# A fused eight-stage transformer kernel on one core: centring folded into weights, the exp mask moved to GpSimd, new interleaving tables

## The reference, cut to what matters

```python
# causal attention, three times (16 heads of 8 features)
scores = einsum('bhqd,bhkd->bhqk', Q, K) / sqrt(dk)
scores = where(causal, scores, NEG)
e = exp(scores - max(scores));  attn = e / e.sum(-1);  out = attn @ V
# the last three blocks
h = x
for blk in range(3):
    y = qlora_linear(h, ..., biases[2*blk])          # w = dequant(q) + lora, plus a bias
    y = layernorm(y, gamma[blk], beta[blk])           # (y - mean(y)) * rsqrt(var + eps) * g + b
    y = gelu(y)
    y = qlora_linear(y, ..., biases[2*blk + 1])
    h = y + h
x = x + h
```

## Time and profile before

| | |
|---|---|
| median of three runs | 3342.96 us (3331.83 to 3349.52) |
| span of the profiled execution, first to last instruction | 3337.4 us |
| device time of the profiled execution | not shown apart; the median is 5.6 us above the span |
| PE busy | 2641.8 us (79%) |
| ACT busy | 1912.7 us (57%) |
| DVE busy | 1763.9 us (53%) |
| POOL busy | 3.6 us |
| mean granted TensorE clock | 0.795 of full speed |

### The profile page before, as it was taken

One profiled execution on the slowest core, in us unless ns is written; L12 is line 12 of the kernel. 1 busy time (PEld: TensorE's weight loads), 2 busy tenths in 40 slices (PEclk: granted clock), 3 DMA queues, 4 the chain that ended last, 5 costly groups with the idle time before them and its releaser, 6 DMA issues.

```text
span 3337.4 us, 46425 instructions
## 1 busy us (share of the span) xinstructions
PE 2641.8 (79%) x18736; PEld 1529.0 (46%) x18736; DVE 1763.9 (53%) x2698; ACT 1912.7 (57%) x1960; POOL 3.6 (0%) x12
## 2 busy tenths in 40 slices
PE   8999999777997789877898688986889868897215
PEld 4666456343563435534355344553445534453102
DVE  5463574545656355553555545654455544563524
ACT  2433435875358753586445864468534685447994
POOL 0000000000000000000000000000000000000000
PEclk7997989659896588966899668986779867987557
DMA  3000000000000000000000000000000000000000
GB/s 128 2 1 1 20 1 1 1 1 8 1 1 1 1 8 1 1 1 0 8 1 1 1 0 8 2 1 1 0 5 2 1 1 0 4 1 1 0 0 6
DMA packets 4561, 18.68 MB, mean 6 GB/s; under 512 B 608, under 2 KB 864, under 8 KB 3808
## 3 DMA queue, kind: packets, MB, share of 16 engines
q1 hardware_dynamic: 4320, 15.38, 1.2%
HBM read 13.28 MB, written 2.10 MB: 5 GB/s over the span
## 4 chain that ended last, share of the span: by engine, by line
PE 54%; ACT 19%; DVE 15%; issue 12%; DVEq 0%; DMA 0%; ACTq 0%; SPq 0%
ACT back_cosines L1320 6%; PE one_ps L1164 2%; PE two_ps L1275 2%; PE one_ps L862 2%; PE two_ps L910 2%; ACT back_cosines L1322 2%; PE one_ps L1710 2%; DVE back_nsum L1330 2%; PE one_ps L1717 2%; ACT L1320 2%; PE one_ps L766 1%; PE one_ps L1723 1%; DVE back_cosines L1393 1%; ACT L1862 1%; PE two_ps L862 1%
## 5 line engine op out<-in xcount | busy, mean ns | idle before, releaser
L1320 ACT ACTIVATE back_cosines<-back_cosines 128x2048 f32<-128x2048 f32 x256 | 472.2, 1899 | 0.5
L933 ACT ACTIVATE front_scratch<-one_ps 128x1152 f32<-128x1152 f32 x168 | 171.5, 1021 | 225.0 <-PE one_ps L848 224.8
L1322 ACT ACTIVATE back_cosines<-back_cosines,wts 128x2048 f32<-128x2048 f32 x128 | 252.4, 1994 | 41.1 <-DVE back_cosines L1393 40.9
L1330 DVE TENSOR_REDUCE back_nsum<-back_cosines 128x8 f32<-128x2048 f32 x64 | 144.4, 2281 | 234.0 <-ACT back_cosines L1320 234.0
L797 DVE TENSOR_REDUCE front_negm<-one_ps 128x8 f32<-128x1024 f32 (+1 forms) x168 | 204.4, 1220 | 56.6 <-PE one_ps L772 55.5
L837 PE MATMUL one_ps<-ident_bf,mask_q 128*128 128x256 bf16 x480 | 93.3, 302 | 80.5 <-ACT front_scratch L933 69.3
L696 ACT ACTIVATE back_cosines<-two_ps,wts 128x512 fp32r<-128x512 f32 x28 | 19.3, 688 | 224.1 <-PE two_ps L910 224.1
L766 PE MATMUL one_ps<-front_qkr 32*128 32x128 f32 (+1 forms) x896 | 136.5, 414 | 14.1 <-issue 8.9
L1393 DVE TENSOR_SCALAR back_cosines<-two_ps 128x2048 f32<-128x2048 f32 x56 | 128.2, 2290 | 28.5 <-PE two_ps L1257 28.3
L933 ACT ACTIVATE back_cosines<-two_ps 128x1152 f32<-128x1152 f32 (+1 forms) x84 | 86.0, 1024 | 92.0 <-PE two_ps L848 92.0
L766 PEld LDWEIGHTS one_ps<-front_qkr 32*128 32x128 f32 x896 | 96.6, 274 | 88.5 <-DVE front_negm L797 46.3
(11 more groups left out here) (630 smaller groups left out, 5795.1 us busy)
## 6 DMA issues: line engine op xcount, KB each, us to landing
wts<-w_dram SPq DMA_DIRECT2D x1, 4184.0 KB, 15.3
front_xin<-x_dram SPq DMA_DIRECT2D x8, 256.0 KB, 4.2
out_dram<-back_z SPq DMA_DIRECT2D x8, 256.0 KB, 2.1
wts<-w_dram SPq DMA_DIRECT2D x1, 1736.5 KB, 19.1
wts<-w_dram SPq DMA_DIRECT2D x1, 1199.0 KB, 5.3
wts<-w_dram SPq DMA_DIRECT2D x1, 1152.0 KB, 16.5
wts<-w_dram SPq DMA_DIRECT2D x3, 256.0 KB, 5.8
wts<-w_dram SPq DMA_DIRECT2D x1, 516.5 KB, 4.8
```

Of the source, the lines that this page charges most:

```text
L933: nc.scalar.activation(h.probs[:, e % 2, 0:n * HEADW].rearrange("p (k c) -> p k c", c=HEADW), h.ps[:, 0:n, 0:HEADW], ACT.Exp, scale=float( ...
L1320: nc.scalar.activation(cosines, cosines, func, scale=scale).then_inc(h.arc_pass.sem, 1)
L1322: nc.scalar.activation(cosines, cosines, func, scale=scale, bias=C(bias)).then_inc(h.arc_pass.sem, 1)
L1330: nc.vector.tensor_reduce(h.nsum[:, kt, :].rearrange("p (g2 j) -> p j g2", g2=2), h.cosines[:, u % 2, kt * 4 * TOK:(kt + 1) * 4 * TOK].rea ...
```

## The change

1. In the causal stages the mask matmuls of the score sets are gone. The exponential is taken of unmasked diagonals, written in another arrangement (for each set, first the tiles of key tile 0 on the diagonal, then the off-diagonal ones, then the other diagonal ones, so that key tile 0 of a head is two pieces 2n tiles apart in PSUM order and n tiles in SBUF order), and GpSimd then sets what lies above the diagonal to zero with one `affine_select` for each set over the 2n diagonal tiles. A new semaphore `probs_kept` stands between GpSimd and the PV matmuls. The scores of the next set still wait for `probs_ready` of ACT alone.
2. In the three blocks the first weight is centred once (`weff` minus its mean over the output features), and its bias with it. The bias step on DVE and the centring matmul of each block go; ACT squares the PSUM result with the centred bias added, and DVE adds the bias in the normalising product. The prologue gets one small matmul, one copy, one reduction and one more pass over half of `weff`. The DMA of the `qlora` parameters is issued ahead of `lora` and gets a semaphore of its own.
3. All interleaving tables are new, and there is one for GpSimd.

```diff
-         "arccos", "qlora", "block0_in", "block0", "block1_in", "block1", "block2_in", "block2"]
+         "arccos", "qlora", "block0", "block1", "block2"]
...
-    "block0": ("y", "xn", True, "eps5", "block0_in", None),
+    "block0": ("y", "xn", False, "eps5", None, None),
...
 PE_RUNS = {
     "fronts": (
-        1, 1, 1, 1, 1, 1, 1, 1, 1, 1, 2, 2, 2, 1, 2, 2, 5, 1, 5, 2, 1, 1, 2, 1, 2, 1, 2, 1, 2, 1, 2, 1, 2, 2, 2,
+        1, 2, 1, 1, 1, 1, 1, 1, 1, 1, 1, 1, 1, 1, 2, 1, 2, 1, 2, 1, 3, 1, 5, 1, 1, 1, 1, 1, 2, 1, 6, 1, 3, 1, 1,
...
+POOL_RUNS = {
...
+    "both": (
+        12, 12, 12,
+    ),
...
+        def score_tile(h, k, kt):
+            return h.ps[:, k, 0:HEADW].rearrange("p (n q) -> p n q", q=P)[:, 0:3:2, :] if kt == 0 else h.ps[:, k, P:2 * P]
+
+        def prob_tile(h, e, k, kt):
+            n = TRIOS[e % len(TRIOS)]
+            tiles = h.probs[:, e % 2, 0:n * HEADW].rearrange("p (t k q) -> p t k q", k=n, q=P)
+            return tiles[:, 0:3:2, k, :] if kt == 0 else tiles[:, 1, k, :]
+
         def causal_scores_pe(pe, h, turn, s):
...
-                    for k in range(len(heads)):
-                        diagonals = h.ps[:, k, :].rearrange("p (n q) -> p n q", q=P)[:, 0:4:2, :]
-                        nc.tensor.matmul(diagonals, mask_q[:], ident_bf[:].unsqueeze(1).broadcast_to([P, 2, P]),
-                                         start=True, stop=False, skip_group_check=True)
-                    for kt, into in ((0, slice(0, SEQ)), (1, slice(SEQ, HEADW))):
+                    for kt in range(2):
...
         def causal_pv_pe(pe, h, turn, s, e):
...
-            pe.wait_ge(h.probs_ready.sem, h.probs_ready.at(turn, s, e + 1))
+            pe.wait_ge(h.probs_kept.sem, h.probs_kept.at(turn, s, e + 1))
...
-                nc.scalar.activation(h.probs[:, e % 2, 0:n * HEADW].rearrange("p (k c) -> p k c", c=HEADW),
-                                     h.ps[:, 0:n, 0:HEADW], ACT.Exp, scale=float(HD) ** -0.5).then_inc(h.probs_ready.sem, 1)
+                nc.scalar.activation(h.probs[:, e % 2, 0:n * HEADW].rearrange("p (t k q) -> p k t q", k=n, q=P),
+                                     h.ps[:, 0:n, 0:HEADW].rearrange("p k (t q) -> p k t q", q=P), ACT.Exp,
+                                     scale=float(HD) ** -0.5).then_inc(h.probs_ready.sem, 1)
+
+        def causal_keep_pool(pool, h, turn, s):
+            for e in range(CSETS):
+                n = TRIOS[e % len(TRIOS)]
+                yield
+                pool.wait_ge(h.probs_ready.sem, h.probs_ready.at(turn, s, e + 1))
+                pool.sem_inc(wait_carrier)
+                diagonals = h.probs[:, e % 2, 0:2 * n * P].rearrange("p (n q) -> p n q", q=P)
+                nc.gpsimd.affine_select(diagonals, diagonals, pattern=[[0, 2 * n], [1, P]], compare_op=ALU.is_ge, fill=0.0,
+                                        base=0, channel_multiplier=-1).then_inc(h.probs_kept.sem, 1)
...
         def block_pe(pe, h, turn, s):
...
-            yield from norm_pe(pe, h, turn, s)
+            yield
+            pe.wait_ge(h.norm_sq.sem, h.norm_sq.at(turn, s))
+            nc.tensor.matmul(h.ps[:, 1, :], C("mean"), h.sq[:], start=True, stop=True).then_inc(h.norm_var.sem, 1)
...
         def block_act(act, h, turn, s):
...
-            yield from norm_act(act, h, turn, s)
+            yield
+            act.wait_ge(h.lin_ps.sem, h.lin_ps.at(turn, s, 1))
+            nc.scalar.activation(h.sq[:], h.ps[:, 2, :], ACT.Square, bias=centred_bias[:, i:i + 1]).then_inc(h.norm_sq.sem, 1)
...
         def block_dve(dve, h, turn, s):
...
-            dve.wait_ge(h.lin_ps.sem, h.lin_ps.at(turn, s, 1))
-            nc.vector.tensor_scalar(h.y[:], h.ps[:, 2, :], bias[:, 2 * i:2 * i + 1], None, ALU.add).then_inc(h.resid.sem, 1)
-            yield from norm_dve(dve, h, turn, s)
+            yield
+            dve.wait_ge(h.norm_rstd.sem, h.norm_rstd.at(turn, s))
+            nc.vector.scalar_tensor_tensor(out=h.xn[:], in0=h.ps[:, 2, :], scalar=centred_bias[:, i:i + 1], in1=h.sq[:],
+                                           op0=ALU.add, op1=ALU.mult).then_inc(h.norm_out.sem, 1)
...
             load_x(0, slice(2 * TOK, 3 * TOK))
+            load("qlora")
             load("lora")
             sp.dma_start(weff_int[:], qw_dram).then_inc(qint_loaded, 16)
-            load("qlora")
...
+            pe.wait_ge(*weights_of("qlora"))
+            last = nc.tensor.matmul(two_back.ps[:, 1, 2 * P:2 * P + 3], C("centre"), W("qlora", "bias")[:, 0:6:2], start=True, stop=True)
             last.then_inc(lora_ps, 1)
...
-                .then_inc(weff_ready, 1)
+                .then_inc(dequant_step, 1)
+            nc.vector.tensor_copy(centred_bias[:], two_back.ps[:, 1, 2 * P:2 * P + 3]).then_inc(dequant_step, 1)
+            dve.wait_ge(dequant_step, 5)
+            first_linear = weff[:].rearrange("p (n c) -> p n c", c=P)[:, 0:6:2, :]
+            nc.vector.tensor_reduce(weff_sum[:], first_linear, AX.X, ALU.add).then_inc(dequant_step, 1)
+            dve.wait_ge(dequant_step, 6)
+            nc.vector.scalar_tensor_tensor(out=first_linear, in0=weff_sum[:].unsqueeze(2).broadcast_to([P, 3, P]), scalar=-1.0 / P,
+                                           in1=first_linear, op0=ALU.mult, op1=ALU.add).then_inc(weff_ready, 1)
```

More of the change, by code:

```diff
@@ L86 @@
 LOADS = {"const": ("const",), "masks": ("masks",), "first": ("causal0",), "moe0": ("moe0",), "front": ("causal1", "mqa", "moe1"),
-         "lora": ("lora",), "back": ("qlora", "linear"), "late": ("causal2", "mlp", "arccos")}
+         "lora": ("lora",), "qlora": ("qlora",), "back": ("linear",), "late": ("causal2", "mlp", "arccos")}
 def columns():
@@ L294, in __init__ @@
         self.front, self.region, self.passes = parts is FRONT, region, passes
-        if not self.front:
-            stages |= {f"block{i}_in" for i in range(3)}
         norms = [n for kind, n in parts if kind == "norm"] + [n for kind, n in parts if kind == "block"]
@@ L416, in __init__ @@
         self.probs_ready = signal("probs_ready", {s: CSETS for s in CAUSAL} | {"linear": CSETS, "mqa": QSETS})
+        self.probs_kept = signal("probs_kept", {s: CSETS for s in CAUSAL})
         self.token_keys = signal("token_keys", {"linear": 1})
@@ L842, in causal_scores_pe @@
                             keys = slice(b * SEQ + kt * P, b * SEQ + (kt + 1) * P)
-                            nc.tensor.matmul(h.ps[:, k, into], h.k4r[rows(j, QUAD), g, keys], h.q4r[rows(j, QUAD), g, queries],
-                                             start=False, stop=False, skip_group_check=True)
+                            nc.tensor.matmul(score_tile(h, k, kt), h.k4r[rows(j, QUAD), g, keys], h.q4r[rows(j, QUAD), g, queries],
+                                             start=True, stop=False, skip_group_check=True)
                         for k, (b, j) in enumerate(heads):
@@ L847, in causal_scores_pe @@
                             minus_max = max_rows[rows(j, QUAD), g:g + 1].broadcast_to([QUAD, P])
-                            last = nc.tensor.matmul(h.ps[:, k, into], minus_max, h.maxTr[rows(j, QUAD), queries],
+                            last = nc.tensor.matmul(score_tile(h, k, kt), minus_max, h.maxTr[rows(j, QUAD), queries],
                                                     start=False, stop=True, skip_group_check=True)
@@ L1830, in block_act @@
             i = int(s[-1])
-            yield from norm_act(act, h, turn, s)
+            yield
+            act.wait_ge(h.lin_ps.sem, h.lin_ps.at(turn, s, 1))
+            nc.scalar.activation(h.sq[:], h.ps[:, 2, :], ACT.Square, bias=centred_bias[:, i:i + 1]).then_inc(h.norm_sq.sem, 1)
+            yield
+            table(LN_EXP)
+            act.wait_ge(h.norm_var.sem, h.norm_var.at(turn, s))
+            nc.scalar.activation(h.sq[:], h.ps[:, 1, :], ACT.Ln, bias=C("eps5")).then_inc(h.norm_ln.sem, 1)
+            yield
+            table(LN_EXP)
+            act.wait_ge(h.norm_ln.sem, h.norm_ln.at(turn, s))
+            nc.scalar.activation(h.sq[:], h.sq[:], ACT.Exp, scale=-0.5).then_inc(h.norm_rstd.sem, 1)
             yield
@@ L1848, in block_dve @@
             out, done = (h.z, h.resid) if i < 2 else (h.y, h.lin_sum)
-            nc.vector.scalar_tensor_tensor(out=out[:], in0=h.ps[:, 3, :], scalar=bias[:, 2 * i + 1:2 * i + 2],
+            nc.vector.scalar_tensor_tensor(out=out[:], in0=h.ps[:, 3, :], scalar=W("qlora", "bias")[:, 2 * i + 1:2 * i + 2],
                                            in1=h.z[:], op0=ALU.add, op1=ALU.add).then_inc(done.sem, 1)
@@ L1930, in _ @@
             nc.gpsimd.memset(spare[:], 0.0).then_inc(out_stored, 16)
+            run(pool, POOL_RUNS, {"norm": nothing_pool, "causal": headed_pool, "linear": headed_pool, "mqa": nothing_pool,
+                                  "moe0": nothing_pool, "moe1": nothing_pool, "mlp": nothing_pool, "arccos": nothing_pool,
+                                  "block": nothing_pool})
         CONSTS = 19
```

24 lines of the change are left out of this document (18 added, 6 removed), and 75 rows, old and new, of tables (ACT_RUNS, DVE_RUNS, PE_RUNS).

## The result

The changed kernel took 3460.31 us (median of four runs, 3454.67 to 3464.89) against 3339.53 us before; the ratio is 1.035 [1.0318, 1.0382]. The forecast was 3252 us, 2.7% faster. It is 3.5% slower, far outside the range of 3190 to 3345.

What follows compares the result with a forecast made beforehand. PE was taken to bound the causal stages and ACT arccos and part of the last section. Terms of -96.6, +25, -18.4, +1.3, +7.7 and -10 summed to -91 us, 3343 to 3252 us; range 3190 to 3345.

Steps and rivals of the forecast that it cites:

- Term A: Causal stages: removing the mask matmuls from PE saves 96.6 us, with half of causal1's counted; bounds 82.8 to 110.4.
- Term B: Causal stages: PE's PV matmuls waiting for the GpSimd select, taken as 1.38 us for 768 elements, cost 25 us.
- the formula: In Term B, two sets take 2.86 + W + t us: W the other half's work between, t the select.
- the slower rival: GpSimd bounds the causal stages, with a select of 3.0 us: 3411 us; chance 0.13.
- Term C: The three blocks: dropping centring matmul and bias step saves 18.4 us, 12.4 in the loop and 6 at the end.
- Terms D and E: D: DVE's one-time weight centring before the loop, +1.3 us. E: ten more table loads in the last section, +7.7 us.
- Term F: All interleaving tables: the new order itself gains 10 us; bounds 30 us either way.
- The rivals: All hidden, 3189 us (0.15); select takes the masks' place, 3325 us (0.15); GpSimd bounds the causal stages, 3411 us (0.13).
- three signs of being wrong: Selects over 2 us, an exponential longer than 1.13, or a turn shrinking although PE waits for GpSimd in every set.

Runs made afterwards that it cites:

- select_only: The kernel before with the GpSimd select in place of the mask matmuls, old tables, blocks uncentred; 3340.6 us, 0.9998.
- mixed_uncentred: The kernel before with the select in causal0 and causal2, mask matmuls kept in causal1, old tables, no centring; 3323.2 us, 0.9952.
- old_tables: The changed kernel (select, centred weights) with the interleaving tables of before, empty steps where a block lost one; 3342.7 us, 1.0007.
- tail_new: `old_tables` with a turn's steps from the start of mqa on in the new order, no empty block steps in the loop; 3365.6 us, 1.0103.
- middle_new: `old_tables` with a turn's steps from the start of arccos to the start of mqa in the new order; 3368.1 us, 1.0102.
- fill_full: `old_tables` plus two zero matmuls of 128 columns in 7 of 12 sets of each causal stage; 3346.2 us, 1.0022.
- fill_linear: `old_tables` plus one zero matmul of 128 columns in 7 of 12 sets of the linear attention; 3358.0 us, 1.0045.
- mixed_front: `mixed_uncentred` with masks by matmul in the last section too; 3315.1 us, 0.9914.
- centring_only: The kernel before with the centred weights alone: masks by matmul, old tables with empty steps; 3347.5 us, 1.0028.
- mixed: `old_tables` with masks by matmul again in causal1, the select serving causal0 and causal2; 3327.5 us, 0.996.
- head_later_new: `old_tables` with a turn's steps from the end of linear to the start of arccos in the new order; 3390.2 us, 1.015.
- new_tables_masks: The changed kernel with the mask matmuls back on PE and no select, new tables and centred weights kept; 3488.0 us, 1.0442.
- fill_rows: `fill_full` with zero matmuls of 32 output columns instead of 128; 3354.9 us, 1.006.

## Why the prediction was wrong

**Term A, -96.6 us, measured about 0.** This is the first step that failed. The 0.42 us of a mask were real, but I took the rate of all other matmuls as given and booked a shorter PE as a shorter section. The stretches of causal0 and causal2 show what happened instead. The kernel before and `select_only`, at the same place of a turn, 92 to 133 us in:

```profile
903.00:944.10 41.10, 38.86 (x450) 24.35 (x449) 20.83 (x50) 20.31 (x24) 0.00 (x0) 1.00 0.01 2
```

```profile
1303.90:1345.00 41.10, 37.19 (x424) 24.29 (x422) 22.94 (x49) 20.33 (x24) 12.94 (x15) 0.92 0.01 2
```

PE was 95% busy at 1.00, that is at 2.4 GHz throughout; with the masks gone it pauses more, is 90% busy, and has 1.2 GHz for part of the time. Over the whole execution PE's busy time in `select_only` is 40 us under the 2641.8 of the earlier trace rows, and not 110, and the span is the same:

```profile
PE 2601.3 (78%) x17968; PEld 1503.8 (45%) x17968; DVE 1773.7 (53%) x2698; ACT 1910.2 (57%) x1960; POOL 236.9 (7%) x300
```

By this account the rest of the 110 went into slower matmuls, and the 40 into waiting. In causal1, from 221 to 271 us of a turn, before and `select_only`, then `mixed_uncentred`, which has its masks there:

```profile
1031.80:1081.80 50.00, 34.01 (x385) 19.02 (x386) 27.35 (x28) 37.11 (x26) 0.00 (x0) 0.74 0.00 1
```

```profile
1432.70:1482.70 50.00, 33.54 (x352) 18.70 (x352) 25.10 (x24) 34.31 (x26) 9.43 (x12) 0.65 0.01 1
```

```profile
1426.40:1476.40 50.00, 34.74 (x391) 19.88 (x389) 27.98 (x26) 36.89 (x29) 0.00 (x0) 0.77 0.00 1
```

0.74 and 0.77 with masks, 0.65 without. The Trainium skill's page TensorE: Matmul & The Clock Gate (A second HAM failure mode: psum-queue depth-cycling) tells of a kernel in which short idle times of PE between groups of matmuls made the clock go back and forth; these rows agree. The stage takes 45.5, 48.6 and 45.2 us by the table. I had counted half of causal1's masks as gain (13.8 us in six turns); their removal is a loss of 3 us a turn.

Over the profiled executions the account is this. First section, old order: four with masks took 401.6 to 409.9 us, mean 406.8, nine without 388.5 to 410.5, mean 398.0: 9 us gained of my 18.4. Last section, from the last block of the loop on: five with masks 479.1 to 484.2, mean 481.2, eleven without 479.3 to 498.7, mean 489.3: 8 us lost where I had 9.2 gained. Turn: 408.9 against 408.7 for `select_only`. Together -2 us, and `select_only` measures 0. How much the clock decides shows where nothing else differs. The first section is the same program in `old_tables`, `tail_new` and `middle_new`:

```profile
0.00:398.00 398.00, 361.19 (x2627) 229.99 (x2628) 216.88 (x409) 143.68 (x200) 41.22 (x60) 0.87 0.07 28
```

```profile
0.00:388.00 388.00, 346.61 (x2626) 222.14 (x2626) 216.42 (x407) 143.57 (x200) 41.22 (x60) 0.91 0.07 28
```

```profile
0.00:410.00 410.00, 370.46 (x2626) 234.30 (x2626) 217.06 (x407) 143.76 (x200) 41.23 (x60) 0.84 0.07 27
```

388 us, my forecast for this section, came true once, at 0.91. That the clock is a cause and not only a sign of idle time rests on `fill_full` (more work, higher clock, same time), on causal1 in `mixed_uncentred` and on linear in `fill_linear`, where added work made a stage shorter, and more weakly, one execution against one, on the last section in `mixed_front`. Not shown: how much of the missing 97 us is the clock's and how much belongs to chains that do not run through the masks, and why PE's clock differs between executions of the same first section.

**Term B, +25 us, measured 0 to about 10.** The select is 0.87 us in the median, inside my bounds, and near the low end of them the formula gives little. The 14 long ones lie above my bound of 2.03; what they overlap with, DVE at work on SBUF, I had only named as a reason for the slower rival. The 1.66 us estimated from the Trainium skill's GPSIMD Engine Reference (Performance versus the Vector engine) was further off than my 1.38. It stands for work on two inputs and a select has one, so it was not a price for this instruction. Term B was right in kind, too high, and without effect on the miss.

**Term C, -18.4 us.** The end was right: from block0's first matmul to the end took 47.5 us before, 41.5 in `centring_only` and in `mixed`: 6.0. In the changed kernel it is 42.7, with the Square right behind the first weight's matmul, which answers to the earlier trace rows:

```profile
3420.80 1.13 PE L1859 MATMUL two_ps<-back_z,weff 128*128 128x512 f32 x2 [0.84 <-DVE back_z L1898]
...
3421.96 0.69 ACT L1873 ACTIVATE back_sq<-two_ps,centred_bias 128x512 f32<-128x512 f32 x1 [0.53 <-PE two_ps L1859]
```

The 12.4 us in the loop did not come, and `centring_only` was no faster as a whole: 0.789 of clock against 0.797. Two more pairs that differ by the centring alone say the same: `old_tables` 1.0007 and `select_only` 0.9998, `mixed` 0.9960 and `mixed_uncentred` 0.9952. Centring on top of `mixed_front` was not tried. Where its 12 us in the loop went was not followed.

**Terms D and E.** D is too small to be seen. The last section has its ten more table loads, ACT busy 342.1 against 327.7 us. I counted six of them, 7.7 us; how much of this section's 29 us (508.2 in the changed kernel, 479.3 in `old_tables`) they are was not separated from the rest of the order.

**Term F, -10 us, measured +118 (with masks, +140).** The second and largest failure. Bounds of 30 either way had come from one wait of 4.62 us in causal1. That wait was not what held a turn: `middle_new` gives causal1 the new order, causal1 gets 5.7 us shorter, and the turn does not. By the table, `head_later_new` and `tail_new`, a turn is held by the back half's chain into arccos on ACT, and by mqa filling PE under it. Against `old_tables` the new order starts arccos 5.6 us later and has 100 of mqa's matmuls behind it instead of 31; mqa ends 16.0 us later and the turn 9.5. The long selects are no part of this, since `new_tables_masks` has none and loses more. In the profiled executions 68 us of the loss are the loop's, 29 the last section's and 15 the first's; only the loop was taken apart, and the same first section varies by 22 us with the clock. Arccos' delay and mqa's place both stood in the orders. I had looked at counts, and at places where PE waits, but not at what moved ahead of arccos' first activation.

**The rivals.** My slower rival named POOL as the bound at t = 3.0 us; the time came out on its side of the range, and its mechanism is refuted by a select of 0.88 us. None of the rivals was an order that is worse in itself, or a clock that falls with the work removed, and of my three signs of being wrong none looked at either.

## What to carry to other kernels

Before an engine's work is removed, look at the granted clock of the stretch and ask what PE does in the freed time: a pause there may cost what the removal gives, and where another engine is the bound the work was free. Price a new order by the start of the stage that fills the next engine (here arccos on ACT), one milestone at a time, and give it bounds of several per cent when most rows move. Test parts of a turn apart, but do not add them up.

## What the runs showed of the hardware that was not expected

- Matmuls of zeros at 14 a stage, 336 in all (111 us busy in `fill_rows`), left the ratio at 1.0022 and 1.006 against the 1.0007 of `old_tables`, and raised the run's mean clock from 0.776 to 0.785, in their full-width form to 0.794.
- The same first section took 388.5 to 410.5 us in different programs, by a clock of 0.91 to 0.84.
- A select in place of 128x768 floats took 0.87 us in the median and of 128x512 0.64 us, on either buffer. Beside DVE's two operations over 2048 elements in moe0 the same selects took 2.1 to 2.7 us, 14 of 14 in the changed kernel, and the second of these operations took 2.83 us in each of the six turns, against 2.28 in the kernel before.
- A busy PE is not always one at full clock. From 31 to 51 us of the second turn of the kernel before, with linear's and the max part's matmuls side by side, PE was 88% busy at 0.50 (columns as in the earlier trace rows). A few matmuls of zeros among them (`fill_linear`) brought the like stretch to 0.71:

```profile
841.50:862.00 20.50, 17.95 (x138) 9.96 (x132) 14.53 (x15) 1.38 (x2) 0.00 (x0) 0.50 0.00 1
```
